# All eight weight folds ahead of the first expert layer, ScalarE's copies and roots in another order, one top-k round in a gap of VectorE, and the second half's adjacency one step sooner

## The reference, cut to what matters

```python
# stage 1: adjacency attention over ctx_512
sim = einsum('bhnd,bhmd->bnm', Q, K) / (sqrt(d) * H)        # 256 x 256 per batch
threshold = top_k(sim, 76)[0][:, :, -1:]                    # the 76th largest of each row
A = sigmoid(sim) * (sim >= threshold)
adj = (1 - gamma) * norm(x) + gamma * 0.5 * (A + A^T)
x = x + tanh(g_xattn[0]) * adj
# stage 2: 8 experts, 2 per token, and a shared one
x = x + tanh(g_ffn[0]) * (sum_e combine_e * down_e(silu(gate_e) * up_e) + shared)
# stage 3: latent attention, 16 heads; stage 4: 16 experts, 2 per token
```

## Time and profile before

| | us |
|---|---|
| median of 3 runs | 545.96 (545.31 to 547.03) |
| profiled execution, its own time | 546.06 |
| its span, first to last instruction | 543.9 |
| PE busy in the span | 496.7 (91%) |
| DVE busy | 415.2 (76%) |
| ACT busy | 308.6 (57%) |
| POOL busy | 280.3 (52%) |
| chain that ended last | PE 65%, DVE 21%, ACT 4%, issue 3%, DMA 3% |

### The profile page before, as it was taken

One profiled execution on the slowest core, in us unless ns is written; L12 is line 12 of the kernel. 1 busy time (PEld: TensorE's weight loads), 2 busy tenths in 40 slices (PEclk: granted clock), 3 DMA queues, 4 the chain that ended last, 5 costly groups with the idle time before them and its releaser, 6 DMA issues.

```text
span 543.9 us, 9155 instructions
## 1 busy us (share of the span) xinstructions
PE 496.7 (91%) x2775; PEld 382.8 (70%) x2775; DVE 415.2 (76%) x1060; ACT 308.6 (57%) x789; POOL 280.3 (52%) x291
## 2 busy tenths in 40 slices
PE   6886999998997997789999999999998977999996
PEld 3664678876876885557777777777776756778874
DVE  4998599988477658888999999999997874644322
ACT  3744554433644643267877777787777772155541
POOL 0042446765433842658777778786661016436560
PEclk9969799999999999879999999999999996999998
DMA  7659313322422319944727180807004602334426
GB/s 255 206 187 302 135 50 93 87 62 59 145 85 62 88 39 227 180 109 96 150 55 170 36 192 11 193 10 166 1 2 186 290 5 84 107 105 127 127 64 231
DMA packets 40281, 65.02 MB, mean 120 GB/s; under 512 B 4324, under 2 KB 30638, under 8 KB 39985
## 3 DMA queue, kind: packets, MB, share of 16 engines
q1 hardware_dynamic: 37984, 60.31, 39.4%
q0 software_dynamic: 2256, 4.21, 2.4%
HBM read 38.48 MB, written 27.99 MB: 122 GB/s over the span
## 4 chain that ended last, share of the span: by engine, by line
PE 65%; DVE 21%; ACT 4%; issue 3%; DMA 3%; POOL 1%; another core or an unknown queue 1%; SPq 1%; POOLq 0%; DVEq 0%
PE bank L1588 10%; PE bank L802 9%; PE bank L1643 5%; PE bank L1632 5%; PE bank L1662 5%; PE bank L1006 5%; PE bank L837 4%; PE bank L1605 3%; PE bank L1609 3%; PE bank L1622 3%; PE bank L1623 2%; PE bank L1022 2%; DVE xn L359 2%; DVE hid L758 2%; DVE silu L756 2%
## 5 line engine op out<-in xcount | busy, mean ns | idle before, releaser
L1423 POOL TENSOR_TENSOR qr<-qr 128x512 f32<-128x512 f32 x48 | 61.6, 1283 | 15.9 <-DVE qr L2078 15.9
L2078 DVE TENSOR_TENSOR qr<-bank,sinq 64x512 f32<-64x512 f32 x96 | 66.1, 689 | 2.2
L1815 ACT ACTIVATE silu<-bank,negm 128x256 f32<-128x256 f32 x128 | 59.2, 470 | 5.9 <-DVE negm L2092 5.9
L719 POOL TENSOR_TENSOR ffn_w_l<-ffn_raw,ffn_w_h 128x512 fp32r<-128x512 f32 x30 | 39.4, 1315 | 35.3 <-ACT ffn_w_h L731 35.2
L1428 POOL TENSOR_TENSOR hid<-silu,rden 128x256 f32<-128x256 f32 x55 | 33.7, 613 | 36.4 <-DVE rden L2097 36.4
L743 ACT ACTIVATE hid_h<-hid 128x512 fp32r<-128x512 f32 x28 | 17.7, 631 | 55.5 <-DVE hid L758 49.2
L2092 DVE TENSOR_REDUCE negm<-bank 128x2 f32<-128x512 f32 x64 | 44.2, 691 | 6.4 <-PE bank L1623 3.7
L1822 ACT ACTIVATE hid<-silu,rden 128x256 f32<-128x256 f32 x55 | 27.9, 507 | 34.2 <-DVE rden L2097 34.2
L961 POOL DMA_INDIRECT y_rows<-moe_y,route_rows x31 | 30.1, 971 | 30.7 <-issue 16.8
L802 PE MATMUL bank<-xT_h,ffn_w_h 128*128 128x512 f32 x120 | 41.4, 428 | 2.9 <-DVE xT_l L416 2.9
L1828 ACT ACTIVATE probsT<-bank 128x512 f32<-128x512 f32 x64 | 37.9, 592 | 10.1 <-PE bank L1632 9.7
(11 more groups left out here) (255 smaller groups left out, 1395.2 us busy)
## 6 DMA issues: line engine op xcount, KB each, us to landing
xn_slots<-blank SPq DMA_DIRECT2D x8, 2056.0 KB, 12.5
ffn_raw<-in_w_ffn SPq DMA_DIRECT2D x30, 256.0 KB, 2.7
pair_w<-in_pair_w SPq DMA_DIRECT2D x8, 768.0 KB, 5.2
moe_w<-in_w_moe SPq DMA_DIRECT2D x1, 6144.0 KB, 17.9
moe_x<-xn_slots SPq DMA_DIRECT2D x31, 128.5 KB
ffn_raw<-in_w_ffn SPq DMA_DIRECT2D x30, 128.0 KB, 2.4
folds<-att_w_raw SPq DMA_DIRECT2D x6, 640.0 KB, 7.5
att_w_raw<-folds SPq DMA_DIRECT2D x6, 384.0 KB, 12.1
```

The source lines that it names most:

```text
L719: nc.gpsimd.tensor_tensor(wt_l[b][:, 0:GU], raw[b][:, 0:GU], wt_h[b][:, 0:GU], ALU.subtract).then_inc(self.wgl, 1)
L1423: nc.gpsimd.tensor_tensor(qr[n][:, 0, :], qr[n][:, 0, :], qr[n][:, 1, :], ALU.add).then_inc(s_turned, 1)
L1815: last = nc.scalar.activation(ex[u % 2][:, h, :], bank[4 + u % 2][:, h * S:(h + 1) * S], ACT.Exp, bias=negm[:, u % 2, h:h + 1], accum_out= ...
L2078: last = nc.vector.tensor_tensor(by_sin[other, :, :], q2[hs, :, :], sinq[hs, j:j + 1, :].broadcast_to([C, 2, S]), ALU.mult)
```

## The change

The arithmetic stays, but for two tiles of the second half's norm, which ACT now applies as scale and shift. What changes is where things stand in the streams.

- **PE.** Folds 5 and 6 stand ahead of `add_transposed(1, 6)`, fold 7 right behind it, so all eight are ahead of the transposes of the first expert layer's norm. Before, fold 5 stood behind `add_transposed` and folds 6 and 7 behind the first `gateup`. The second half's adjacency transposes move from hook 9 to hook 8.
- **ACT.** The roots of the first norm stand behind the two `pT` copies, with a table load of their own. `fold_out(1)` stands behind the first pair of sigmoids instead of behind all four, the gate constants and the roots; `fold_out(5)`, `fold_out(6)` ahead of the root of `n_ffn0[0]`, `fold_out(7)` behind its `act_high`. A one-column square root into `table_out` is new. Hook 11 is `act_apply` of the second half's norm, new.
- **DVE.** Reciprocal and Newton step of the first norm are done once for all 8 tiles, ahead of `topk(0)`; `stats` of the first batch stand between the two updates. Round 0 of the second half's search stands ahead of the first `hid`, rounds 1 and 2 behind `route0_choose`, and `AHEAD` is 3. `threshold_second_half`, the two updates and `refine_second_half` are hooked one step sooner, and two of the four `xn` tiles are left to ACT.
- `Norm.shared` becomes the count of tiles or shifts that is waited for (1 for norm 1, 2 for norm 5).

```diff
         self.i, self.hf, self.banks = i, hf, banks
-        self.by_bits, self.roots, self.shared = roots is None, roots, i == 5
+        self.by_bits, self.roots, self.shared = roots is None, roots, {1: 1, 5: 2}.get(i, 0)
         self.var, self.root, self.ln, self.tr, self.h, self.l = sems_of
...
-        act.wait_ge(self.shift, 1)
+        act.wait_ge(self.shift, self.shared)
         for t in (4 * self.hf + 2, 4 * self.hf + 3):
...
         for t in (4 * self.hf, 4 * self.hf + 1):
-            ins = nc.vector.tensor_scalar(xn[:, t, :], x[:, t, :], mv[:, t, 0:1], rstd[:, t:t + 1],
-                                          ALU.subtract, ALU.mult)
-        ins.then_inc(self.ln, 1)
+            nc.vector.tensor_scalar(xn[:, t, :], x[:, t, :], mv[:, t, 0:1], rstd[:, t:t + 1],
+                                    ALU.subtract, ALU.mult).then_inc(self.ln, 1)
...
         if self.shared and g:
-            eng.wait_ge(self.part, 1)
+            eng.wait_ge(self.part, self.shared)
         else:
-            eng.wait_ge(self.ln, 2 * self.i + g + 1)
+            eng.wait_ge(self.ln, 2 * self.i + (2 if self.shared else g + 1))
...
 n_l0att = [Norm(first_norm, hf, hf, None, hf + 1) for hf in range(2)]
+n_l0both = Norm(first_norm, 0, 0, None, 2)
+n_l0both.tiles = slice(0, NT)
 n_ffn0 = [Norm(later_norm, hf, hf, ((5, 6), (6, 7))[hf], (1, None)[hf]) for hf in range(2)]
...
 s_top, s_rep = sems("topk", "eight_found", "eight_taken")
-AHEAD = 2
+AHEAD = 3
 kth, rounds = (TOPK - 1) % 8, (TOPK + 7) // 8
...
         fold(4)
+        fold(5)
+        fold(6)
         add_transposed(1, 6)
-        fold(5)
+        fold(7)
         n_ffn0[0].pe_transpose(pe)
...
         route[0][0].pe_turn_logits(pe)
-        fold(6)
-        fold(7)
         pe.wait_ge(s_fcp, 4 * (NPAIR - 1) + KD)
...
         ffn0.prog_pe(pe, {1: lambda: rows_pe(route[0][0], pe),
-                          N0 - 5: transposed_second_half,
+                          N0 - 6: transposed_second_half,
                           N0 - 2: lambda: n_ffn0[1].pe_transpose(pe),
...
                                  ACT.Copy).then_inc(s_ctc, 1)
+            n_l0att[c].act_root(act)
         def similarity_out(g):
...
         act.wait_ge(s_gates, 48)
-        nc.scalar.activation(tg[:, 4:5], gates[:, 4:5], ACT.Sigmoid).then_inc(s_gact, 1)
-        for g in range(NT // 2):
+
+        def sigmoid(g):
             nc.scalar.activation(sig[:, 2 * g:2 * g + 2, :], sim[:, 2 * g:2 * g + 2, :],
                                  ACT.Sigmoid, scale=1.0 / 16.0).then_inc(s_sig, 1)
+
+        nc.scalar.activation(tg[:, 4:5], gates[:, 4:5], ACT.Sigmoid).then_inc(s_gact, 1)
+        sigmoid(0)
         nc.scalar.activation(tg[:, 0:4], gates[:, 0:4], ACT.Tanh).then_inc(s_gact, 1)
+        fold_out(1)
         act.wait_ge(s_rg, 48)
...
         nc.scalar.activation(rg_h[:], rg_raw[:], ACT.Copy).then_inc(s_gact, 1)
-        for hf in range(2):
-            n_l0att[hf].act_root(act)
+        for g in range(1, NT // 2):
+            sigmoid(g)
         act.wait_ge(s_zz, 1)
         nc.scalar.activation(zero[:], hid[0][:], ACT.Copy)
-        for i in range(1, 4):
+        fold_out(2)
+        fold_out(3)
+        ffn0.first_splits(act)
+        for i in range(4, NPAIR - 1):
             fold_out(i)
-        ffn0.first_splits(act)
-        fold_out(4)
+        nc.scalar.activation(table_out[:, 0:1], tg[:, 0:1], ACT.Sqrt)
         n_ffn0[0].act_root(act)
-        fold_out(5)
         n_ffn0[0].act_high(act)
+        fold_out(NPAIR - 1)
         route[0][0].act_logits(act)
...
         ffn0.act_high(act, ffn0_first)
-        fold_out(NPAIR - 2)
-        fold_out(NPAIR - 1)
...
         ffn0.prog_act(act, {1: lambda: rows_act(route[0][0], act),
+                            N0 - 3: lambda: n_ffn0[1].act_apply(act),
                             N0 - 2: lambda: n_ffn0[1].act_high(act), N0 - 1: lambda: route[0][1].act_logits(act),
...
+        n_l0both.invert(dve, seq)
+        n_l0both.refine(seq)
         topk(0)
...
         seq.link(nc.vector.tensor_scalar(cc[:, 2:3], cc[:, 0:1], 0.5, None, ALU.mult))
-        n_l0att[0].scale(dve, seq)
+        n_l0att[0].apply(seq)
         topk(1)
...
         update(0, 5)
+        dve.wait_ge(s_upd, 1)
+        n_ffn0[0].stats(seq, 0)
         update(1, 6)
         dve.wait_ge(s_upd, 2)
-        n_ffn0[0].stats(seq)
+        n_ffn0[0].stats(seq, 1)
         n_ffn0[0].scale(dve, seq)
...
         n_ffn0[0].low(dve)
-        n_l0att[1].scale(dve, seq)
-        ffn0.hidden(dve, ffn0_first)
-        route0_shift(route[0][0], dve, seq)
-        ffn0.low(dve, nc.vector, ffn0_first)
-        route0_choose(route[0][0], dve, seq)
+        n_l0att[1].apply(seq)
         dve.wait_ge(s_left, NT // 2)
...
             n_ffn0[1].refine(seq)
-            n_ffn0[1].apply(seq)
+            n_ffn0[1].shifts(seq)
+            n_ffn0[1].apply_first(dve)
...
-        for r in range(AHEAD):
+        find_eight(0)
+        take_eight(0)
+        ffn0.hidden(dve, ffn0_first)
+        route0_shift(route[0][0], dve, seq)
+        ffn0.low(dve, nc.vector, ffn0_first)
+        route0_choose(route[0][0], dve, seq)
+        for r in range(1, AHEAD):
             find_eight(r)
...
         ffn0.prog_dve(dve, {2: lambda: dve.wait_ge(route[0][0].rowc, 1),
-                            N0 - 6: threshold_second_half,
-                            N0 - 5: lambda: update_second_half(0), N0 - 4: lambda: update_second_half(1),
-                            N0 - 3: refine_second_half, N0 - 2: lambda: n_ffn0[1].low(dve), N0: sum_first_half, N0 + 1: lambda: route0_choose(route[0][1], dve, seq),
+                            N0 - 7: threshold_second_half,
+                            N0 - 6: lambda: update_second_half(0), N0 - 5: lambda: update_second_half(1),
+                            N0 - 4: refine_second_half, N0 - 2: lambda: n_ffn0[1].low(dve), N0: sum_first_half, N0 + 1: lambda: route0_choose(route[0][1], dve, seq),
                             N0 + 2: second_rows, N0 + 3: lambda: n_att[0].invert(dve, seq), N0 + 4: lambda: n_att[0].refine(seq),
```

## The result

| | before | changed |
|---|---|---|
| median of 4 runs | 546.25 | 552.57 (552.07 to 553.49) |
| profiled execution, its own time | 546.06 | 552.07 |
| its span | 543.9 | 550.3 |

The change makes the kernel slower: by 6.3 us by the medians, and by 5.7 by the ratio on record, 1.0105 (95% interval 1.0085 to 1.0125), which isn't formed from the two medians (their quotient is 1.0116). 552.57 is outside the predicted range of 542.5 to 549.2, and on the side of the second rival.

The account below looks back on a forecast made before the run. It took the folds' waits for loads, the join before stage 2 (adjacency, update, norm, `xn` transposes) and VectorE's rounds to bound the first 140 us. Sum: 546.06 + 2.4 - 1.0 - 1.0 - 1.1 = 545.36, say 545.4; range 542.5 to 549.2.

Parts of the forecast that it names:

- the second rival: Folds on TensorE: clock falls in the idle 2.6 before fold 5, giving 548.0 to 549.0; chance 0.29.
- Folds, the term +2.4: Join before stage 2: folds waiting for loads delay TensorE's transposes of `xn` from 52.48 to 54.9, +2.4.
- its bound (+5.2): Join: with all loads at 7.4 + 0.4, fold 7 would end at 57.7, +5.2.
- The clock between folds: TensorE idle 2.6 before fold 5 drops the clock; slow folds 5 and 6 put the update at 53.6; chance 0.29.
- Clock in the router's logits and first gate-up, -1.0: TensorE behind the folds: if full clock held, 5.68 of busy time would be 2.84 shorter; taken as -1.0.
- Round in the gap, 0: VectorE's idle 5.04 before the first `hid` product takes a search round of 3.14: cost 0, up to 1 if uncovered.
- Steps, -1.0: First steps: folds 6 and 7 no longer hold up TensorE, so VectorE's silu waits of 0.44 and 0.54 go, -1.0.
- Second half's norm, -1.1: Second half: applied a step sooner and half on ScalarE, so TensorE's waits for `xn`, 0.71 and 0.40, go, -1.1.
- The 1.2 taken from between the searches at the start: Start on VectorE: reciprocal and Newton step moved ahead of the first search, so search 1 and its adjacency end about 1.2 sooner.
- The table load: Start on ScalarE: the load costs twice its 1.28, delaying the first search by 0.9; 545.4 to 546.3, chance 0.03.

Follow-up runs that it names:

- e7: Changed kernel plus three filling matmuls, results unread, between folds 4 and 5: 548.83, ratio 1.0101 to the kernel before.
- e14: Repeat on another chip of the changed kernel plus three filling matmuls between folds 4 and 5: 547.93, ratio 1.0094 to the kernel before.
- e15: Repeat of the changed kernel with three filling matmuls between folds 4 and 5 and four ahead of the router's comb transposes: 547.34, ratio 1.0080 to before.
- e2: Changed kernel plus six filling matmuls, results unread, between folds 4 and 5: 548.79, ratio 1.0084 to the kernel before.
- e9: Changed kernel plus three filling matmuls between folds 4 and 5 and four ahead of the router's comb transposes: 546.75, ratio 1.0063 to the kernel before.
- e13: Changed kernel without the loads of pairs 5 to 7, so its output is not the reference's: 541.46, ratio 0.9993 to the kernel before.
- e1: Changed kernel with folds 5, 6 and 7 and ScalarE's copies of them back in their old places: 540.14, ratio 0.9946 to the kernel before.
- e8: Kernel before with the start part alone (early roots and Newton step, early copy of fold 1, split statistics): 541.35, ratio 0.9963 to the kernel before.
- e12: Changed kernel with folds 5 to 7 back in place, plus four filling matmuls ahead of the second adjacency: 539.64, ratio 0.9928 to the kernel before.
- e3: Changed kernel with the second adjacency's transposes between folds 5 and 6 instead of behind 6: 550.13, ratio 1.0107 to the kernel before.
- e10: Changed kernel plus four filling matmuls ahead of the router's comb transposes alone: 548.45, ratio 1.0065 to the kernel before.
- e4: Kernel before with only folds 5, 6 and 7 and ScalarE's copies of them moved ahead: 553.04, ratio 1.0193 to the kernel before.
- e16: Changed kernel unaltered, run again beside other runs on another chip: 548.51, ratio 1.0099 to the kernel before.
- e5: Changed kernel unaltered, run again beside other runs on another chip: 547.60, ratio 1.0103 to the kernel before.
- e6: Changed kernel with fold 5 ahead of the second adjacency, fold 6 behind it, fold 7 behind the first gate-up: 541.59, ratio 0.9965 to the kernel before.

## Why the prediction was wrong

**Folds, the term +2.4: mis-sized, and the step that failed.** It measured +7.0. The mechanism was right: folds wait for their loads, the adjacency for fold 6, the transposes for fold 7. The size was taken from single landings in the old order, 6.6 and 7.3 with the issue's lag. There, folds 6 and 7 stood behind the first gate-up, and their traffic was spread until 62. A fold moves 768 + 160 KB in and 640 KB out, 1.57 MB; at the 301 GB/s of the earlier trace rows that is an estimate of 5.2 us for each fold, whatever TensorE does. From 24.9 on, five loads and the stores of four to five folds lie ahead of fold 7, 7.2 to 7.8 MB, an estimate of 24 to 26 us: fold 7 at 49 to 51 at the earliest, with nothing lost anywhere. The prediction had it at 51.6, with next to no slack, and with landings that took no note of the stores beside them. The estimate is still a little low: in e7, 0.64 MB of expert weights were issued at 48.1 to 49.3, beside the load of fold 7. How full the stretch was shows in e7 too, where the clock held for every fold and fold 7 began at 53.02 (columns as in the earlier trace rows):

```profile
24.90:53.80 28.90, 22.58 (x127) 15.39 (x124) 23.09 (x84) 15.45 (x49) 9.07 (x8) 1.00 0.94 312
```

The DMA engines were 94% busy over the whole stretch. The three runs with fills in which the clock held for all folds (e7, e14, e15) began fold 7 at 53.0 to 53.8 and the transposes at 56.6, 58.0 and 57.1: +4.1 to +5.5 in place of +2.4, the upper end of what the prediction had put as its bound (+5.2). The rest to +7.0 is the clock: 1.5 to 2.9 at the join of the profiled executions, less by the medians. In e2 and e9, whose fills did not keep fold 7 at full clock, the transposes stood at 61.3 and 62.9. e13 shows it from the other side: without three of the loads the same order is 8 us earlier at the join.

**The clock between folds, a rival at 0.29: it came to pass.** The idle was 3.53 instead of 2.6, and the update came at 55.26, where the rival had 53.6. Its time, 548.0 to 549.0, was still too low, for three reasons: the update was 1.7 later than it said, the steps gave back less, and the last stage was 2.2 longer in this execution. Of the 1.7, 1.2 is a slip in its own sum: it lets fold 6 begin at 45.8, when a slow fold 5 (41.1 + 5.87) runs until 47.0, so fold 6 would end at 52.8 and not at 51.7. The fills show that the rival named the visible part and not the root: with the clock kept full the time hardly improves, and the join still loses 4.1 to 5.5. Its reading that one idle time between 1.44 and 4.98 decides doesn't hold either, as the last section shows.

**Clock in the router's logits and first gate-up, -1.0:** +7.00 at the transposes became +5.72 at the first product, -1.3. The size was right and the reason not shown: the prediction put it down to folds that end right ahead of the transposes. From the transposes to the first product it is 10.69 before and 9.41 changed, but also 9.59 in e1 and 9.83 in e8, where folds 6 and 7 haven't moved. Counted from the transposes, the granted clock was back at 1.00 some 3 us sooner in all three than before; why, no run tells. It was luck in part.

**Round in the gap, 0:** right, 2.12 of idle was left before the first product.

**Steps, -1.0:** too high. The waits of 0.44 and 0.54 are gone, but the way from the first product to the second grew by 1.0 (12.72 for 11.72), most of it in one 128x32 product of VectorE (`sc<-sc,rinv`), 1.04 for 0.19. POOL splits a weight beside it, as it did not before; that this is the reason is likely and not tested. From the first to the third silu it is -0.3 in sum (15.66 for 15.93). So folds 6 and 7 filled these gaps of TensorE for a cost of 0.3, and the prediction read them as a delay of 1.0.

**Second half's norm, -1.1:** from the third to the 14th silu -1.15, with no wait for `xn`. Right. The 1.2 taken from between the searches at the start is real too: batch 0's update stands at 44.80 for 45.91. Behind fold 6 that could not show. Nor did it show at the join of e8, where no fold is in the way: the second adjacency begins 0.6 sooner, at 45.41, but after an idle of 3.06 at half clock (1.11 for 0.66), and the transposes stand at 52.49 as before. e8's gain comes behind them, 0.9 of it by the first product. e12 shows what a full clock there is worth.

**The table load:** one of 1.28 and no drain behind it: the root follows at 10.65, a load from 9.35. That rival falls.

**What stays open:** how much the clock costs on top of the loads, which the fills leave between nothing and 3; and what makes the waits for gathered tokens in the last stage vary from one execution to the next. By the ratio the change costs 5.7, 5.6 and 5.4 on three chips, so nothing here points to a difference between chips.

## What to carry to other kernels

When a group of work that loads and stores is moved ahead of a join, add up its bytes and divide by the rate that the full stretch shows, before pricing single landings: a landing read in the old order already has the old spacing in it. Work that stands in an engine's wait for another engine can be nearly free there (0.3 for two folds here), and moving it to the front can turn it into the path; look at what it filled before moving it. The parts of a change that give little each (start -2.2, second half -1.9) are worth running without the one that loses.

## What the runs showed of the hardware

- Between folds, TensorE's clock had fallen after idle times of 3.53 (changed kernel), 3.00 (e3), 2.86 (e10) and 2.45 (e4), where the next first product took 2.79 to 2.93. Before fold 4, idle times of 1.35 (e8), 1.68 (e16), 1.86 (e5 and e9) and 2.39 (e6) went with 2.20, 2.18, 2.39 and 2.63, and 2.14, partly slow; 1.65 to 1.75 (e14, e12, changed) went with 1.57 and 1.95 (e3) with 1.62. Idle times of 2.28 (e8) to 3.06 (e10) before fold 3 left its first product at 1.57. So the same idle time may or may not cost the clock, and the one row that I had for it didn't tell.
- Three to four idle microseconds filled with matmuls kept the clock where the fill began at full clock (e7, e12, e14, e15). Where it began at half clock (e9) the three matmuls took 5.35 for 2.84 and held the next fold up.
- The 16 DMA engines moved 312 GB/s when 94% busy over 28.9 us (e7). A 160 KB load issued behind one of 768 KB landed 7.3 (e1, e15) to 8.6 us (e6) after its issue at 29 to 31 us, in every run in which fold 2 began at 27.2 or sooner; issued at 49.92 it took 4.8 (e12).
- The kernel before itself had medians of 546.25 on the first chip and 543.5 to 544.2 on the others, and single runs from 539 to 548.5: comparisons need the runs on one chip.
